# Attention value matmuls in two column halves of TensorE, row sums from 32-column matmuls of ones

## The reference, cut to what matters

```python
x = (sequence - mean) / jnp.sqrt(var + EPS) * ln_gamma + ln_beta
q, k, v = heads(x @ Wq.T + bq), heads(x @ Wk.T + bk), heads(x @ Wv.T + bv)
scores = jnp.einsum('bhqd,bhkd->bhqk', q, k) / scale          # scale 8
scores = jax.nn.sigmoid(scores - mu) * jnp.exp(scores)
scores = scores / jnp.sum(scores, axis=-1, keepdims=True)
out = jnp.einsum('bhqk,bhkd->bhqd', scores, v)                 # then @ Wo.T + bo
```

## Time and profile before

| | us |
|---|---|
| median of 3 runs (lowest, highest) | 4304.37 (4302.19, 4306.89) |
| the profiled execution, its own time | 4332.54 |
| its span on the slowest core (core 5) | 4330.6 |
| its span on core 0 | 4294.0 |
| ACT busy on core 5 | 3938.9 (91%) |
| PE busy on core 5 | 3749.7 (87%) |
| DVE busy on core 5 | 3343.6 (77%) |

### The profile page before, as it was taken

The page is one execution under the profiler, slowest core; times in us unless marked ns, Lnnn a source line. Parts: engine busy times, 40 slices in busy tenths (PEclk is TensorE's granted clock), DMA queues, the critical chain, the costliest instruction groups (busy, mean ns, idle before and its releaser), DMA issues.

```text
span 4330.6 us, 58783 instructions; the slowest of 8 cores (4292.8 to 4330.6 us)
## 1 busy us (share of the span) xinstructions
PE 3749.7 (87%) x15282; PEld 1540.3 (36%) x15282; DVE 3343.6 (77%) x4049; ACT 3938.9 (91%) x4275; POOL 216.1 (5%) x360
## 2 busy tenths in 40 slices
PE   4567999999999999999988888778777878899994
PEld 3333544444444444443333232222222222222222
DVE  5555788878877888887777788878888898877766
ACT  3667999999999999999999999999999999999970
POOL 0000011101110110010000100000000000000000
PEclk9666788878877887786677786887898879755557
DMA  7543333333433343444544631112112111211110
GB/s 204 164 155 125 112 117 126 112 114 119 126 109 104 114 131 106 125 151 131 141 132 131 136 91 44 44 44 84 44 44 75 53 46 44 64 56 45 47 35 21
DMA packets 251967, 419.13 MB, mean 97 GB/s; under 512 B 30466, under 2 KB 213762, under 8 KB 241412
## 3 DMA queue, kind: packets, MB, share of 16 engines
q1 hardware_dynamic: 226564, 335.68, 26.4%
q0 software_dynamic: 25088, 79.71, 6.0%
HBM read 352.36 MB, written 71.30 MB: 98 GB/s over the span
## 4 chain that ended last, share of the span: by engine, by line
PE 39%; ACT 35%; issue 13%; DVE 11%; DVEq 0%; ACTq 0%; SPq 0%; DMA 0%; POOL 0%
ACT tb L105 26%; PE sc L96 14%; PE bg L96 13%; PE op L96 12%; ACT eb L105 7%; DVE wb L123 6%; ACT xn L105 1%; DVE dn L718 1%; PE bg L101 1%; ACT xnt L105 1%; ACT th L105 0%; DVEq L55 0%; DVE stat L488 0%; ACTq L55 0%; DVE kev L114 0%
## 5 line engine op out<-in xcount | busy, mean ns | idle before, releaser
L123 DVE SCALAR_TENSOR_TENSOR wb<-tb,eb 128x1024 bf16<-128x1024 bf16 x2048 | 2492.9, 1223 | 824.5 <-ACT eb L105 637.9
L105 ACT ACTIVATE tb<-sc 128x1024 bf16<-128x1024 f32 x2048 | 2478.5, 1210 | 100.0 <-PE sc L96 87.6
L105 ACT ACTIVATE eb<-sc 128x1024 bf16<-128x1024 f32 x2048 | 2488.8, 1215 | 0.0
L96 PE MATMUL sc<-qt,kb 67*128 67x512 bf16 x4096 | 1567.5, 473 | 335.4 <-ACT eb L105 325.8
L96 PE MATMUL op<-wb,vb 128*128 128x512 bf16 x4096 | 1595.8, 480 | 24.9 <-DVE s1b L109 23.9
L96 PEld LDWEIGHTS op<-wb,vb 128*128 128x128 bf16 x4096 | 479.2, 118 | 776.6 <-issue 649.0
L96 PEld LDWEIGHTS sc<-qt,kb 67*128 67x128 bf16 x4096 | 344.2, 106 | 1101.5 <-issue 1074.5
L96 PE MATMUL bg<-b_wv,xnt 128*128 128x256 bf16 (+1 forms) x2560 | 346.8, 286 | 66.2 <-DVE kev L114 66.2
L96 PE MATMUL bg<-xnt,b_wk 128*128 128x512 bf16 x1024 | 346.5, 458 | 5.6 <-ACT xnt L105 3.9
L96 PEld LDWEIGHTS bg<-b_wv,xnt 128*128 128x128 bf16 x2560 | 251.7, 113 | 209.1 <-issue 186.0
L96 PEld LDWEIGHTS bg<-xnt,b_wk 128*128 128x128 bf16 x1024 | 115.9, 114 | 170.2 <-issue 167.2
(11 more groups left out here) (149 smaller groups left out, 1630.9 us busy)
## 6 DMA issues: line engine op xcount, KB each, us to landing
vb<-vd SPq DMA_DIRECT2D x512, 192.0 KB, 2.7
kb<-ktd SPq DMA_DIRECT2D x512, 128.0 KB, 3.0
xnt<-xnd SPq DMA_DIRECT2D x64, 1024.0 KB, 5.9
vd<-vev POOLq DMA_DIRECT2D x128, 192.0 KB, 4.9
vxb<-vd SPq DMA_DIRECT2D x128, 192.0 KB, 2.5
xb<-xkv SPq DMA_DIRECT2D x32, 512.0 KB, 4.6
att<-xkv SPq DMA_DIRECT2D x32, 512.0 KB, 4.7
xnd<-xnt POOLq DMA_DIRECT2D x16, 1024.0 KB, 5.0
```

The lines of the kernel that those rows point to most:

```text
L96: return lambda e: e.matmul(out, lhsT, rhs, start=start, stop=stop)
L105: return lambda e: e.activation(out, in_, func, **kw)
L123: return lambda e: e.scalar_tensor_tensor(out, a, s, b, op0=op0, op1=op1)
```

## The change

`values` gives each head a 64-column stationary operand (V alone) in a column half of the array, so that both write one tile, `op0`: head 0 its rows 0 to 63, head 1 its rows 64 to 127. The row sums come from matmuls with 32 columns of ones, four side by side, one for each head of two blocks, and only in every odd block; they write the four quarters of `op1`. So `take_sums` now has an addition (block parity 0 and 1), and `epilogue` takes reciprocals of 64 rows and spreads them over 128 rows by four copies. V is stored without ones (128 columns), and `product` waits for the block pair's last matmul. `extra` loads V into a tile with a 129th column of ones.

```diff
-        s1b = sb(big, "s1b", [128, 512])
+        s1b = sb(big, "s1b", [64, 512])
+        ones = sb(big, "ones", [128, 32], BF16)
...
             def ld_v(i):
...
-                    vx_ok[i] = SP.dma(dVX[i % 4], vxb[i % 4][:], vd[order[i][0], order[i][1]])
+                    vx_ok[i] = SP.dma(dVX[i % 4], vxb[i % 4][:, :, 0:128],
+                                  vd[order[i][0], order[i][1]].rearrange("p (b w) -> p b w", b=4))
...
-                        f = mm(ring.banks[b][0:2, 0:VW], wx[:, 2 * k:2 * k + 2],
-                               vxb[i % 4][:, VW * j:VW * (j + 1)], k == 0, k == KS - 1)
+                        f = mm(ring.banks[b][0:2, 0:129], wx[:, 2 * k:2 * k + 2],
+                               vxb[i % 4][:, j, :], k == 0, k == KS - 1)
...
-                        yield (400, 0)
+                        yield (300, 0)
...
         def product(n):
             DVE.wait((a2, n + 1))
             if n >= NW:
-                DVE.wait((m2, n - NW + 1))
+                DVE.wait((m2, (n - NW + 2) // 2 * 2))
             DVE.sig(stt(wb[n % NW][:], tb[n % 4][:], 1.0, eb[n % 4][:], AX.add, AX.mult), s1)
 
         def values(n):
...
-            for h in range(2):
-                f = mm(op[h][:], vb[G % 4][:, VW * j + 64 * h:VW * j + 64 * h + 128],
-                       wb[n % NW][:, 512 * h:512 * (h + 1)], k == 0, k == KS - 1)
-                if h == 0:
-                    PE.run(f)
-                else:
-                    PE.sig(f, m2)
+
+            todo = [mm(op[0][64 * h:64 * h + 64, :], vb[G % 4][:, 128 * j + 64 * h:128 * j + 64 * h + 64],
+                       wb[n % NW][:, 512 * h:512 * (h + 1)], k == 0, k == KS - 1, (0, 64 * h))
+                    for h in range(2)]
+            if k % 2:
+                PE.wait(tok_ones)
+                todo += [mm(op[1][32 * i:32 * i + 32, :], ones[:],
+                            wb[(n - 1 + i // 2) % NW][:, 512 * (i % 2):512 * (i % 2 + 1)],
+                            k == 1, k == KS - 1, (0, 32 * i)) for i in range(4)]
+            for f in todo[:-1]:
+                PE.run(f)
+            PE.sig(todo[-1], m2)
 
         def take_sums(u):
             DVE.wait((m2, (u + 1) * KS))
             DVE.run(cp(s0[:], op[0][:]))
-            o_ok[0] = DVE.step(cp(s1b[:], op[1][:]))
+            DVE.step(cp(s1b[:], op[1][0:64, :]))
+            o_ok[0] = DVE.step(tt(s1b[:], s1b[:], op[1][64:128, :], AX.add))
 
         def epilogue(u):
             p, c = units[u]
-            yield (0, 1.4)
-            DVE.run(cp(dn[0:64, :], s0[64:128, :]))
-            yield (0, 0.42)
-            DVE.step(cp(dn[64:128, :], s1b[0:64, :]))
-            yield (0, 0.42)
+            yield (0, 2.1)
             for i in range(8):
                 f = slice(64 * i, 64 * (i + 1))
-                tok = DVE.sig(lambda e, f=f: e.reciprocal(dn[:, f], dn[:, f]))
+                tok = DVE.sig(lambda e, f=f: e.reciprocal(s1b[:, f], s1b[:, f]))
                 yield (0, 0.5)
-            a = att_of(p, c)
+            DVE.wait(tok)
+            for i in range(4):
+                tok = DVE.sig(cp(dn[32 * i:32 * i + 32, :], s1b[32 * (i // 2):32 * (i // 2) + 32, :]))
+                yield (0, 0.42)
             DVE.wait(tok, att_rd[c - 3] if c >= 3 and p > 0 else None)
-            DVE.run(tt(a[0:64, :], s0[0:64, :], dn[0:64, :], AX.mult))
-            yield (0, 0.65)
-            att_ok[(c, p)] = DVE.sig(tt(a[64:128, :], s1b[64:128, :], dn[64:128, :], AX.mult))
+            att_ok[(c, p)] = DVE.sig(tt(att_of(p, c), s0[:], dn[:], AX.mult))
             yield (0, 0.65)
```

More of the change, by code:

```diff
@@ L21 @@
 KS = S // 128
-VW = 192
 LAG = 3
@@ L145, in build @@
     ktd = hbm("ktd", [NB, NG, 128, 512])
-    vd = hbm("vd", [NB, NG, 128, 4 * VW])
+    vd = hbm("vd", [NB, NG, 128, 512])
     qd = hbm("qd", [NB, NC, 128, 512])
@@ L189, in build @@
         kb = [sb(big, f"kb{i}", [HR, 2, 512], BF16) for i in range(4)]
-        vb = [sb(big, f"vb{i}", [128, 4 * VW], BF16) for i in range(4)]
+        vb = [sb(big, f"vb{i}", [128, 512], BF16) for i in range(4)]
         qt = [sb(big, f"qt{i}", [HR, 2, 512], BF16) for i in range(2)]
@@ L222, in build @@
         DVE.run(lambda e: e.memset(onef[:], 1.0))
+        tok_ones = DVE.sig(lambda e: e.memset(ones[:], 1.0))
         DVE.run(lambda e: e.memset(qx[:], 0.0))
@@ L277, in build @@
         kev = [sb(first, f"kev{i}", [128, 512], BF16) for i in range(4)]
-        vev = [sb(first, f"vev{i}", [128, 4, 2, VW], BF16) for i in range(2)]
+        vev = [sb(first, f"vev{i}", [128, 4, 2, 128], BF16) for i in range(2)]
         tx = sb(first, "tx", [128, 128], BF16)
@@ L281, in build @@
         wx = sb(first, "wx", [128, 128], BF16)
-        sx = sb(first, "sx", [2, VW])
+        sx = sb(first, "sx", [2, 129])
         rx = sb(first, "rx", [2, 1])
@@ L288, in build @@
         wok = {}
-        for i in range(2):
-            tok_ones = DVE.sig(lambda e, i=i: e.memset(vev[i][:, :, :, 64:128], 1.0))
         nev = [0, 0]
@@ L378, in proj_v @@
                         yield (270 if np_ == 2 else 180, 0)
-                DVE.wait(tok, (dVE[e], dVE[e].v) if dVE[e].v else None, tok_ones)
+                DVE.wait(tok, (dVE[e], dVE[e].v) if dVE[e].v else None)
                 if np_ == 2:
@@ L383, in proj_v @@
                     dst = vev[e][:, :, 0, :]
-                dst = dst.rearrange("p m (t x) -> p m t x", t=3)[:, :, 0:3:2, :]
-                src = ring.banks[b].rearrange("p (m t x) -> p m t x", m=4, t=2)
-                ring.free[b] = DVE.sig(cp(dst, src))
+                ring.free[b] = DVE.sig(cp(dst, ring.banks[b].rearrange("p (m w) -> p m w", m=4)))
                 yield (0, 0.7)
@@ L604, in extra @@
                 b = ring.take()
-                PE.wait(ring.free[b], tok_w)
+                PE.wait(ring.free[b], tok_w, tok_vx)
                 for g in range(NG):
@@ L617, in extra @@
                             vx_rd[i] = PE.sig(f)
-                        yield (400, 0)
+                        yield (300, 0)
                 DVE.wait(vx_rd[i])
-                ring.free[b] = DVE.step(cp(sx[:], ring.banks[b][0:2, 0:VW]))
-                DVE.step(lambda e: e.reciprocal(rx[:], sx[:, 64:65]))
+                ring.free[b] = DVE.step(cp(sx[:], ring.banks[b][0:2, 0:129]))
+                DVE.step(lambda e: e.reciprocal(rx[:], sx[:, 128:129]))
                 tok = DVE.sig(ts(sx[:], sx[:], rx[:], None, AX.mult))
@@ L628, in extra @@
                 PE.run(mm(ring.banks[b][:, 0:1], sx[:, 0:128], idf[0:2, 0:1], True, True))
-                tok = PE.sig(mm(ring.banks[b][:, 1:2], sx[:, 64:192], idf[0:2, 1:2], True, True))
+                tok = PE.sig(mm(ring.banks[b][:, 1:2], sx[:, 0:128], idf[0:2, 1:2], True, True))
                 yield PAUSE
@@ L800, in build @@
         kxb = [sb(first, f"kxb{i}", [128, 512], BF16) for i in range(4)]
-        vxb = [sb(first, f"vxb{i}", [128, 4 * VW], BF16) for i in range(4)]
+        vxb = [sb(first, f"vxb{i}", [128, 4, 129], BF16) for i in range(4)]
+        DVE.wait(*pro_end)
+        for t in vxb:
+            tok_vx = DVE.sig(lambda e, t=t: e.memset(t[:, :, 128:129], 1.0))
         jobs.append(passes())
```

## The result

The changed kernel takes 4522.24 us (median of 4 runs, 4474.91 to 4575.02) against 4305.63 us (4 runs, 4302.19 to 4319.09): a ratio of 1.0391, 95% interval 1.0352 to 1.0429.

A forecast was written before the change was run, and what follows sets the result against it. The prediction took ACT's two activations, about 1.83 us a block, as the bound. Its terms, 10 + 4 + 6 + 8 + 8 + 3 = 39 us, on 4304 gave 4343 us, with a range from 4290 to 4460.

The forecast's parts named there:

- Columns saved, side by side: PE's values and sums: halves and quarters run side by side, 0.32 us a block for 0.43, saving 0.11 at full clock.
- Tile changes at 0.10 us: PE, between matmuls of different tile shape: each change costs about 0.10 us, 2.5 a block, so 0.25 us, 0.28 at half clock.
- The choice that the prediction called its own: PE's tile changes: going from 128 to 64 columns costs as much as 128 to 32, with bounds nothing and 0.13 us.
- Full clock, 10 us: Units 1 to 11: PE's block grows from 1.57 to 1.71 us, mostly hidden under 1.83; 10 us, bounds 0 and 25.
- Half clock with background, 18 us: Blocks with background at half clock: PE takes 0.07 us more on 1.9 to 3 us; 4, 6 and 8 us by stage.
- Half clock without background, nothing: Blocks without background at half clock: PE goes from 1.72 to 1.79 us, still under 1.83, so no cost.
- Change of unit, 8 us: Between units: the added addition takes about 0.76 us more, hidden at full clock, not at half; 8 us, bounds 0 and 24.
- DVE's epilogue, 3 us: End of each unit: more copies and one addition give DVE +0.84 us a unit, mostly covered by ACT; 3 us, at most 8.
- Rival 3: Whole kernel: tile changes make PE wait less at half clock, full clock returns sooner, so faster, 4271 us; chance 0.12.
- Rival 4: PE's weight loads, four a block on average, each show 0.05 us; 4449 us in all; chance 0.16.
- Rival 5: PE's halves and quarters do not run side by side; a full block takes 2.25 us, near 4640 in all; chance 0.09.
- rival 2: Whole kernel: ACT's pace hides everything or the clock makes up for it, within 9 us of 4304; chance 0.17.

The follow-up runs named there:

- e3: Kernel before, with the second head's value matmul left out in every second block and no tile changes added: 4351.42 us, ratio 1.0057.
- e8: Kernel before plus two tile changes a block, by a one-column zero matmul ahead of each block's first value matmul, all columns kept: 4567.41 us, no ratio.
- e10: Kernel before with the second head's value matmul left out in every second block and 2.5 tile changes a block added: 4509.85 us, ratio 1.0468.
- e12: Kernel before with two tile changes a block, as in e8, and the zero filler matmuls of e6: 4374.90 us, ratio 1.0143.
- e6: Kernel before plus one or two zero matmuls of 512 columns (filler) in blocks with little background: 4268.66 us, ratio 0.9903.
- e2: Kernel before with all its columns, plus 2.5 tile changes a block by one-column zero matmuls: 4692.49 us, ratio 1.0634.
- e5: Changed kernel, but values of two blocks are done together in the odd block, 1.5 tile changes a block in place of 2.5: 4480.61 us, ratio 1.0380.
- e1: Changed kernel, but take_sums copies all 128 rows of op1 at once and the halves are added in the epilogue: 4482.48 us, ratio 1.0387.
- e9: Changed kernel with the filler of e7 and the early release of op1 of e1: 4408.54 us, ratio 1.0233.
- e7: Changed kernel plus the same zero filler matmuls as e6, all 2.5 tile changes a block kept: 4508.52 us, ratio 1.0308.
- e11: Kernel before with the filler of e6, placed by the background's real columns so that it also stands in units 13 to 17: 4304.74 us, ratio 0.9955.

## Why the prediction was wrong in size

Direction and prices on PE were right, the size was not: +39 us forecast, some +168 measured (0.0391 of 4305.63). That is about 4472 us, above the upper end of the range, 4460.

**The step that failed** is the one that took the time at half clock, 159, 272, 394 and 414 us, as given. The prediction multiplied the new costs of a block with the clock of the old kernel. The clock followed the change. On core 0 the time at half clock went from 1446 us over the whole span to 1838 in e3 (fewer columns), 1937 in e8 (two tile changes), 2238 in the changed kernel and 2260 in e10 (both). So the missing columns add some 390 us (up to 470 on other cores of e3), two tile changes 490, and both together about 800.

They do not cost the same, because a block at half clock costs nothing as long as PE fills less than ACT's pace. In e3 a block at half clock has less to do, and 0.6% is all that it costs. In e8 each such block has two changes more, and core 0 takes 188 us more. e12 splits these: 92 us are left with filler (4350.7 against e6's 4258.7), of which 73 lie in the one stage whose clock stayed low. The loss is the product of the two: tile changes that make PE the bound at half clock, and half clock of which more comes with the tile changes and with the missing columns. Of the two parts of the change the tile changes carry the loss. With all columns kept, 2.5 of them cost 6.3% (e2); leaving columns out beside them lengthens half clock and yet brings this down to 4.7% (e10) and in the changed kernel to 3.9%. e5, with one change a block fewer and the same time, is the run that this account does not explain outside units 28 to 31.

**The terms.**
- *Columns saved, side by side*: right (0.34 and 0.33 us, of which about 0.12 are the change). The estimate from the figure of 2.38 for three column tiles (the Trainium skill, "TensorE: Matmul & The Clock Gate", Part 3) isn't borne out for two and four: by it the four quarters would last 0.30 us and a change, and they last 0.33 with it. Its price in the prediction, 15 us, was also too low by its own terms: at half clock the difference of 0.07 is 0.14 a block, 46 us on the 327 blocks counted above.
- *Tile changes at 0.10 us*: right, 0.09 to 0.12 at full clock and 0.12 to 0.14 at half, 128 to 64 columns like 128 to 32. The choice that the prediction called its own came true.
- *Full clock, 10 us*: e12 against e6 shows 20 us for two changes in units 1 to 11, with all columns, within the bounds of 0 and 25.
- *Half clock with background, 18 us*: this is the term that was mis-sized. PE's price was near (1.81 us without background for a forecast 1.79), but 632 blocks in units 1 to 27 lie wholly at half clock in place of 327, and they lie 145 us further above ACT's pace.
- *Half clock without background, nothing*: 8 us in units 28 to 31, near enough. The mean of 1.81 leaves 0.02 us below ACT's 1.83.
- *Change of unit, 8 us*: PE waits 25.3 us more for `s1b` in all, 1.4 us a unit where 1.7 was forecast; e1 shows no measurable loss, e9 against e7 0.75%, some 32 us, with intervals that overlap.
- *DVE's epilogue, 3 us*: no view shows a loss there, and no run tried it alone.

**The rivals.** Rival 3 asked the right question, whether the clock would follow, and had the sign wrong. It argued that a PE with fewer waits gets full clock back sooner. PE did wait less (180.5 us for `eb`, not 484.6), and the clock still fell. Its own counter-argument, that fewer columns stream, is what e3 confirms. A rival with that sign and this size was missing. Rival 4 is refuted by starts some 3 ns apart and a group's length of one matmul: the second and later loads of a group add nothing. The rule behind it ("TensorEngine Tiling (Array Packing)" in the Trainium skill, Restrictions and Gotchas, no Fast Weight Load with column tiles) adds no time here beyond the tile change. The first load of a group is another matter. It starts with its matmul and lasts 0.12 us on average for 64 columns and 0.10 for 32 (not the estimated 0.053 and 0.027), about as long as a change costs, and the first load after the change back to the whole array also starts only with its matmul (1149.17). So the 0.10 us of a change may be this load; no run separates the two. Rival 5 is refuted by the same starts, rival 2 by the ratio.

**Left open.** Why the clock did not return while PE was busy without a pause is not settled. Half clock grew in e3, with fewer columns, and in e8, with tile changes, and shrank in e6, with added matmuls; since PE was busy for 398 of 400 us at half clock in e8, its busy time alone does not explain it. Nor is it settled why e5 gained nothing in units 1 to 27, and what a change of tile consists of.

## What to carry to other kernels

Treat TensorE's clock as an outcome of the change, not as a property of the stage: where the profile shows both levels, work out the sum once for each and add a case in which blocks move from one to the other. Packing matmuls side by side saved columns here but paid about 0.10 us for each change of tile shape, so count the changes: here 0.11 us a block was saved and 0.25 paid. That it pays where many packed matmuls follow each other is to be expected from these prices, but was not run. Where another engine sets the pace and the profile shows PE at its lower clock, zero matmuls in PE's spare time may be worth a try; here they gave 1.0% to the kernel before, and more of them (e11) gave no more.

## What the runs showed of the hardware that was not expected

- A PE that is busy for 398 of 400 us stayed at 1.2 GHz all that time when two tile changes stood in each block (e8), and for 131 of 136 us in the changed kernel.
- Leaving out a quarter of the value matmuls made the kernel slower, 1.0057, with core 0 at half clock for 1838 us in place of 1446.
- Adding matmuls of zeros made it faster, 0.9903, with the clock at 0.94 on core 0.
- Four matmuls of 32 columns' width start some 3 ns apart and end after the time of one.
- After a change of tile the first weight load starts with its matmul (1148.50), while between scores and values in the whole array it starts 0.22 us ahead (2162.36 for 2162.58).
- With more filler (e11) core 0 was at half clock for only 303 us, but at 0.81 for 1775.
- A change of tile costs nearly the same time at both clocks (0.09 to 0.12 and 0.12 to 0.14 us), for 64 and for 32 columns' width.
